# Graph-network kernel, convolution at seven points: VectorE's and ScalarE's order of work in each period and in the first group's preparation rearranged

## The reference, cut to what matters

```python
# layer 0
h = relu(bn1(conv1d(xc, conv1_w, 0)))                  # xc = x transposed, one tap
x_conv = relu(bn2(conv1d(h, conv2_w, 8)) + xc)          # 17 taps
s = x @ w_se.T + b_se                                   # 3 columns
A = exp(-(sq[:, :, None] + sq[:, None, :] - 2 * s @ s.T)) * adj
x_nmp = A @ relu(x @ w_msg.T + b_msg)
gi = concat([x_conv, x_nmp]) @ w_ih.T + b_ih
gh = x @ w_hh.T + b_hh                                  # three gates each: r, z, n
r, z = sigmoid(gi_r + gh_r), sigmoid(gi_z + gh_z)
x = layernorm(x + (1 - z) * tanh(gi_n + r * gh_n) + z * x)
# layer 1
h = relu(((1 + eps) * x + adj @ x) @ W1 + b1)
x = layernorm(x + h @ W2 + b2)
```

## Time and profile before

| | us |
|---|---|
| median of 3 runs | 428.92 (428.90 to 428.99) |
| the profiled execution, its own time | 428.78 |
| its span, first to last instruction | 427.0 |
| TensorE matmuls busy | 371.3 (87%) |
| VectorE busy | 315.6 (74%) |
| ScalarE busy | 226.4 (53%) |
| GpSimd busy | 208.2 (49%) |
| mean granted TensorE clock | 0.982 of full |

### The profile page before, as it was taken

The page is one execution under the profiler, slowest core; times in us unless marked ns, Lnnn a source line. Parts: engine busy times, 40 slices in busy tenths (PEclk is TensorE's granted clock), DMA queues, the critical chain, the costliest instruction groups (busy, mean ns, idle before and its releaser), DMA issues.

```text
span 427.0 us, 6485 instructions
## 1 busy us (share of the span) xinstructions
PE 371.3 (87%) x2191; PEld 321.3 (75%) x2191; DVE 315.6 (74%) x671; ACT 226.4 (53%) x421; POOL 208.2 (49%) x195
## 2 busy tenths in 40 slices
PE   3798699889987999789988899879997899898974
PEld 2577688779775987779777797769886797778864
DVE  5999986778777686768767787776957687774574
ACT  3324546455745367453763557553674537533674
POOL 4729522556227562368325661285523583256243
PEclk9799699999999999999999999999999999999999
DMA  7400021020012010120110200120101201000011
GB/s 248 165 1 2 0 100 50 6 94 26 26 49 100 2 51 0 51 98 0 49 49 8 90 25 25 49 98 2 50 2 49 100 2 51 1 2 0 2 49 49
DMA packets 7991, 19.39 MB, mean 45 GB/s; under 512 B 672, under 2 KB 5024, under 8 KB 6944
## 3 DMA queue, kind: packets, MB, share of 16 engines
q1 hardware_dynamic: 7536, 18.50, 12.2%
q10 hardware_dynamic: 432, 0.59, 0.4%
HBM read 14.90 MB, written 4.19 MB: 45 GB/s over the span
## 4 chain that ended last, share of the span: by engine, by line
PE 30%; DVE 24%; issue 20%; POOL 13%; ACT 11%; DMA 1%; DVEq 0%; ACTq 0%; POOLq 0%; SPq 0%
PE back L1213 16%; POOL rstd L515 4%; PE back L1309 4%; PE conv L1213 4%; PE back L1398 3%; DVE bv L858 3%; DVE xn L1005 3%; POOL av L494 2%; POOL av L492 2%; DVE usum L918 2%; DVE usum L949 2%; ACT amat L656 2%; POOL sv L502 2%; DVE stats L983 1%; DVE msg L880 1%
## 5 line engine op out<-in xcount | busy, mean ns | idle before, releaser
L1213 PE MATMUL conv<-sth,wh 128*128 128x256 f32 x238 | 74.8, 314 | 5.3 <-issue 5.3
L1213 PE MATMUL conv<-stl,wh 128*128 128x256 f32 x238 | 69.0, 290 | 0.0
L1213 PE MATMUL conv<-sth,wl 128*128 128x256 f32 x238 | 68.8, 289 | 0.0
L520 POOL TENSOR_TENSOR xw<-xw,xv 128x512 f32<-128x512 f32 (+1 forms) x17 | 20.8, 1224 | 83.2 <-ACT xw L680 83.2
L515 POOL TENSOR_TENSOR rstd<-rstd,minus_half 128x4 f32<-128x4 f32 (+1 forms) x34 | 34.2, 1006 | 54.9 <-DVE rstd L987 54.9
L533 POOL TENSOR_TENSOR amat<-amat,adjT 128x512 f32<-128x512 f32 x32 | 48.2, 1528 | 16.7 <-ACT amat L656 16.7
L1213 PEld LDWEIGHTS conv<-sth,wh 128*128 128x128 f32 x238 | 46.2, 194 | 7.1 <-issue 5.6
L1213 PEld LDWEIGHTS conv<-stl,wh 128*128 128x128 f32 x238 | 46.4, 195 | 0.5
L1213 PEld LDWEIGHTS conv<-sth,wl 128*128 128x128 f32 x238 | 46.1, 194 | 0.0
L614 ACT ACTIVATE sth<-sv 128x272 fp32r<-128x272 f32 (+1 forms) x35 | 18.1, 518 | 36.3 <-DVE sv L834 21.7
L1309 PE MATMUL back<-adjT,xn 128*128 128x256 f32 x120 | 29.9, 392 | 5.8 <-DVE xn L1005 5.8
(11 more groups left out here) (219 smaller groups left out, 1019.2 us busy)
## 6 DMA issues: line engine op xcount, KB each, us to landing
adjT<-in_adj_dram SPq DMA_DIRECT2D x8, 1024.0 KB, 4.9
out_dram<-tail SPq DMA_DIRECT2D x15, 256.0 KB, 2.2
xv<-in_x_dram SPq DMA_DIRECT2D x7, 512.0 KB, 3.3
gbuf<-in_gates_dram SPq DMA_DIRECT2D x1, 576.0 KB, 6.5
tail<-in_conv_dram ACTq DMA_DIRECT2D x2, 256.0 KB, 3.9
xv<-in_x_dram SPq DMA_DIRECT2D x2, 256.0 KB, 4.6
later_w<-in_later_dram SPq DMA_DIRECT2D x1, 452.0 KB, 6.3
tail<-in_conv_dram SPq DMA_DIRECT2D x1, 320.0 KB, 5.2
```

What stands on the lines that cost most here:

```text
L520: done(pool.tensor_tensor(xw[:, h, part(c)], xw[:, h, part(c)], xv[u][:, part_cols(h, c)], ALU.mult), XWX_READY)
L1213: ins = pe.matmul(bank, a, b, start=first and k == 0, stop=last and k == len(todo) - 1)
```

## The change

The number of instructions of each engine stays as it was, but for two copies that go from VectorE to ScalarE; all else is order. SyncE's list is untouched; GpSimd's and TensorE's change in the preparation alone.

- Every period, VectorE: `messages` and `factors` come ahead of `parts1`, and `u_sum` stands behind `inf_stream`, ahead of `gates(gb, 1)`; `gates_end(gb, 0)` comes ahead of `stream_low(gm, 3)`; `gates_end(gb, 1)` and `y_apply(gb, 0)` and `y_stats(gb, 1)` ahead of `pair2_sum`; `stream_low(gm, 4)` and `pair2_add` behind `y_apply(gb, 1)`; `h_low(gb, 0)` ahead of `pair1_sum`; both `x_low` ahead of both `pair1_add`.
- Every period, ScalarE: `xconv_high(gm, 0)` stands behind the four `hidden` instead of ahead of `exps` 2 and 3.
- Preparation: the two copies of the last tap (L1085, L1086) go to ScalarE with a semaphore of their own; on VectorE the sums of the +2 and -2 taps, the messages, factors, streams and low parts stand in another order; the low parts of w1, MINUS2, MINUS1 and INF go into the first period, around `gates_end(0, 0)` and behind `y_stats(0, 0)`. TensorE's first taps go HALF, ZERO, PLUS2, MINUS2 (which was behind `factors`), and INF ahead of `nmp(0, 0)`. TensorE's first `gates` wait for the low part of the gate weights (w1's before), and its taps MINUS2 for all low parts, as before.

```diff
-        W_ORDER = ("conv1", ZERO, HALF, PLUS2, PLUS1, "gates", "w1", MINUS2, MINUS1, INF)
+        W_ORDER = ("conv1", HALF, ZERO, PLUS2, PLUS1, "gates", "w1", MINUS2, MINUS1, INF)
...
 # GpSimd, prologue
                 pool.wait_ge(pads_zeroed, 2)
+                token_diffs(0, 1)
+                streams2(0)
                 pool.wait_ge(conv2_loaded, 64)
                 pool.tensor_tensor(ataps[:, 10:14, :], c2raw[:, 0:16:4, :], c2raw[:, 2:16:4, :],
                                    ALU.add).then_inc(tap_sums_one, 1)
-                token_diffs(0, 1)
...
-                streams2(0)
...
 # ScalarE, prologue
+                act.wait_ge(conv2_loaded, 64)
+                last_tap = c2raw[:, TAPS - 1:TAPS, :]
+                act.activation(gtaps[:, 4:15:5, :], last_tap.to_broadcast([P, 3, P]), ACT.Copy).then_inc(tap_copies, 1)
+                act.activation(ataps[:, 4:10:5, :], last_tap.to_broadcast([P, 2, P]), ACT.Copy).then_inc(tap_copies, 1)
...
 # ScalarE, steady
-                xconv_high(gm, 0)
                 exps(gm, 2)
                 exps(gm, 3)
                 hidden(gb, 0)
                 hidden(gb, 1)
+                xconv_high(gm, 0)
...
 # VectorE, prologue
-                dve.tensor_copy(gtaps[:, 4:15:5, :], last_tap.to_broadcast([P, 3, P])).then_inc(tap_sums, 1)
-                dve.tensor_copy(ataps[:, 4:10:5, :], last_tap.to_broadcast([P, 2, P])).then_inc(tap_sums, 1)
...
+                tap_low(PLUS1)
+                w_low_part(wl[:, S_GATE:S_GATE + 9, :], graw, wh[:, S_GATE:S_GATE + 9, :], w_count("gates"))
...
-                tap_low(MINUS2)
-                tap_low(MINUS1)
-                tap_low(INF)
 
             def steady(s, u, front):
                 gb, gm, gf = s - 1, s, s + 1
-                parts1(gm)
-                u_sum(gm, u)
+                first = isinstance(s, int) and s == 1
                 for k in range(3):
                     messages(gm, k)
                 factors(gm)
+                parts1(gm)
                 gates(gb, 1 - u, 0)
+                if first:
+                    w_low_part(w1l[:, :], w1raw, w1h[:, :], w_count("w1"))
+                    tap_low(MINUS2)
+                gates_end(gb, 0)
                 stream_low(gm, 3)
-                gates_end(gb, 0)
                 inf_stream(gm)
+                u_sum(gm, u)
                 gates(gb, 1 - u, 1)
                 y_stats(gb, 0)
-                pair2_sum(gm)
+                if first:
+                    tap_low(MINUS1)
+                    tap_low(INF)
                 gates_end(gb, 1)
                 y_apply(gb, 0)
+                y_stats(gb, 1)
+                pair2_sum(gm)
+                y_apply(gb, 1)
+                stream_low(gm, 4)
                 pair2_add(gm)
-                y_stats(gb, 1)
-                stream_low(gm, 4)
-                y_apply(gb, 1)
+                h_low(gb, 0)
                 pair1_sum(gm)
-                h_low(gb, 0)
                 h_low(gb, 1)
-                pair1_add(gm, 0)
                 if front:
                     x_low(gf, 1 - u, 0)
                     x_low(gf, 1 - u, 1)
+                pair1_add(gm, 0)
                 pair1_add(gm, 1)
...
 # TensorE, prologue
+                first_taps(HALF)
                 first_taps(ZERO)
-                first_taps(HALF)
                 first_taps(PLUS2)
+                first_taps(MINUS2)
                 pe.wait_ge(consts_loaded, 16)
                 factors(0)
-                first_taps(MINUS2)
...
+                first_taps(INF)
                 nmp(0, 0)
-                first_taps(INF)
                 nmp(0, 1)
...
 # TensorE, steady
                 if first:
-                    pe.wait_ge(w_low, w_count("w1"))
+                    pe.wait_ge(w_low, w_count("gates"))
```

More of the change, by code:

```diff
@@ L314, in gnn_kernel @@
         tap_sums_one = sem("tap_sums_one")
+        tap_copies = sem("tap_copies")
         def wait(eng, name, g, j):
@@ L723, in prologue @@
                 h1_out(0, 1)
[L724 removed]
+                act.wait_ge(tap_copies, 2)
+                act.wait_ge(tap_sums, 3)
+                tap_high(HALF)
                 tap_high(ZERO)
[L726 to L727 removed]
+                x_high(1, 1)
+                act.wait_ge(tap_sums, 6)
+                tap_high(PLUS2)
                 for k in range(3):
                     msg_out(0, k)
[L730 to L732 removed]
+                act.wait_ge(tap_sums_one, 3)
+                tap_high(PLUS1)
                 factors_out(0)
+                minus2_out(0)
                 exps(0, 0)
                 exps(0, 1)
[L736 removed]
+                act.wait_ge(gates_loaded, 16)
+                act.activation(wh[:, S_GATE:S_GATE + 9, :], graw, ACT.Copy).then_inc(w_high, 1)
                 exps(0, 2)
                 exps(0, 3)
[L739 to L742 removed]
                 act.activation(w1h[:, :], w1raw, ACT.Copy).then_inc(w_high, 1)
@@ L746, in prologue @@
                 h1_out(1, 1, True)
+                act.wait_ge(tap_sums, 7)
+                tap_high(MINUS2)
                 xconv_high(0, 0)
@@ L753, in prologue @@
                 xconv_high(0, 1)
-                act.wait_ge(tap_sums, 9)
-                tap_high(MINUS2)
                 act.wait_ge(tap_sums_one, 4)
@@ L1032, in out_shift, with w_low_part, tap_low @@
                                               ALU.mult, ALU.mult), SHIFT_READY)
+            def w_low_part(dst, src, hi, k):
+                dve.wait_ge(w_high, k)
+                dve.tensor_tensor(dst, src, full(hi), ALU.subtract).then_inc(w_low, 1)
+            def tap_low(n):
+                k = SLOT[(n, 0)]
+                w_low_part(wl[:, k:k + NTAP[n], :], traw[n], wh[:, k:k + NTAP[n], :], w_count(n))
             def prologue():
@@ L1095, in prologue @@
                     messages(0, k)
-                taps_step(utaps[:, 0:4, :], w2, 4.0, w0)
-                taps_step(ataps[:, 5:9, :], w3, 4.0, w1)
-                taps_step(gtaps[:, 5:9, :], ataps[:, 5:9, :], 2.0, utaps[:, 0:4, :])
+                factors(0)
                 taps_step(ataps[:, 5:9, :], ataps[:, 5:9, :], -2.0, utaps[:, 0:4, :])
                 parts1(0)
-                factors(0)
-                tap_low(ZERO)
-                tap_low(HALF)
+                inf_stream(0)
+                x_low(1, 1, 0)
+                x_low(1, 1, 1)
                 dve.wait_ge(tap_sums, steps[0])
                 u_sum(0, 0)
-                x_low(1, 1, 0)
-                x_low(1, 1, 1)
-                tap_low(PLUS2)
-                inf_stream(0)
                 pair2_sum(0)
+                tap_low(HALF)
+                tap_low(ZERO)
                 pair2_add(0)
-                tap_low(PLUS1)
-                w_low_part(wl[:, S_GATE:S_GATE + 9, :], graw, wh[:, S_GATE:S_GATE + 9, :], w_count("gates"))
-                w_low_part(w1l[:, :], w1raw, w1h[:, :], w_count("w1"))
                 pair1_sum(0)
                 pair1_add(0, 0)
+                tap_low(PLUS2)
                 pair1_add(0, 1)
@@ L1119, in prologue @@
                 zero_stream(1)
-                xconv_low(0, 0)
                 stream_low(1, 0)
@@ L1242, in first_taps @@
                 elif n == HALF:
-                    pe.wait_ge(tap_sums, 5)
+                    wait(pe, E_READY_H, 0, 1)
+                    pe.wait_ge(tap_copies, 2)
+                    pe.wait_ge(tap_sums, 3)
                 elif n == PLUS2:
                     wait(pe, R2_READY, 0, 2)
-                    pe.wait_ge(tap_sums, 8)
+                    pe.wait_ge(tap_sums, 6)
                 elif n == MINUS2:
-                    pe.wait_ge(tap_sums, 9)
+                    pe.wait_ge(tap_sums, 7)
                 elif n == PLUS1:
```

31 lines of the change are left out of this document (8 added, 23 removed).

## The result

The changed kernel takes **397.35 us** (396.49 to 398.25, four executions) against 428.96 (428.90 to 429.50, four) on the same chip: a ratio of **0.926, 95% interval 0.923 to 0.929**. The forecast was 399.0 in 393 to 407. The profiled execution took 396.49, with a span of 394.7 and a mean granted clock of 0.990; the span before was 427.0.

The account below looks back on a forecast made before the run. TensorE's list plus its waits, 4.55 us in a steady period, was taken to bound the kernel. 428.78 - 29.0 (periods) - 4.7 (preparation) + 3.8 (first period) = 398.9, hence 399.0 us, in 393 to 407.

Parts of the forecast that it names:

- the periods: All periods together: TensorE's 31.1 us of waits go, less a new 0.3 us wait seven times: -29.0 us.
- the preparation: Before the periods: VectorE's first stream of group 1 starts at 39.8 instead of 44.47, -4.7 us (bounds -2.5 and -5.5).
- the first period: Low parts moved into it make TensorE wait before taps MINUS2: +3.8 us (bounds 2.8, 5).
- The new wait at the first INF tap: In a period, TensorE waits for INF's `stl`, now behind pair 1's xn: 0.3 us, bounds 0 and 0.6.
- step 6: From `conv1(gf, 1)` to the next messages: order unchanged, and TensorE follows without a gap as before.
- Steps 1 and 2: Pair 0's gates lose their 0.81 to 0.93 us wait; moved VectorE work makes L969 0.2 us late, with no TensorE wait.
- Step 3: Before the transpose of pair 1's y: TensorE's 1.51 us wait goes, with 0.9 us to spare.
- Step 5: At `mlp1`: the 1.45 us wait before the fourth tile goes; `x_low` and `pair1_add` have over 1 us to spare.
- VectorE becomes the bound: Rival: moved `parts1` and `u_sum` delay the path to the transposes by 4.86 us each period, 433 us; slower: 0.04.
- No wait stayed off another cause: Rival: `mlp1` or the gates still wait for something else, 404 to 409 us; chance 0.19 shared with ports.
- GpSimd's masks did not hold the preparation to 402: Rival: GpSimd's masks set the preparation's pace, so it gives only -2.5 us: 402 us; no separate chance given.
- The port rival: VectorE's moved `pair2_add` and GpSimd hold each other up, delaying `h_low` before `mlp1`: 406 us; 0.19 shared with one wait left.

Follow-up runs that it names:

- experiment 5: The changed kernel with only `pair2_sum` put back ahead of `gates_end(gb, 1)` on VectorE: 410.43 us, ratio 0.956.
- Experiment 4: The changed kernel with only `parts1` and `u_sum` put back ahead of the messages on VectorE: 402.0 us, ratio 0.937.
- experiment 7: The changed kernel with only `pair1_add(gm, 0)` put back ahead of both `x_low` on VectorE: 400.83 us, ratio 0.934.
- experiment 1: The kernel before with the change's order in the periods only, its preparation kept: 395.54 us, ratio 0.922.
- experiment 11: The changed kernel with the first period's low parts spread and the preparation's -2 taps sum ahead of the messages: 394.83 us, ratio 0.921.

## Why the prediction was right, and where its terms were off

The mechanism was right: the waits named in the earlier trace rows went, and the time went with them. That the total came so near is in part luck, since the terms were off in both directions: the periods gave 3.6 us more than forecast in the spans, the preparation 1.2 more, and the first period cost 2.3 more.

- *The bound* was read rightly. TensorE's list sets the period; take its waits away and the period shrinks by them.
- *The periods* were forecast at -29.0 us, with a mark every 45.2 to 45.4. Alone they gave 33.5 (32.6 in the spans of the profiled executions), a mark every 44.8 to 44.9. The new wait at the first INF tap came and was rightly sized: about 0.2 us for 0.3, though it is in no list. Two things were mis-sized. A removed wait gives more than its listed length: some 5.5 us in a period for the 4.55 listed, 1.7 for 1.5 in experiment 5. And a second new wait of some 0.5 us, before the second `HALF` taps, was not foreseen: step 6 had TensorE without a gap there.
- *Steps 1 and 2* held. Experiment 4 puts the order of messages and `parts1` at 4.7 us in all, though its wait in the first period is 2.0 us shorter, so at some 6.7 us by itself, or 0.96 in each period; the earlier trace rows list 0.8 to 0.9. `parts1` takes 1.14 us in its new place. I had taken 2.21 as its time beside GpSimd, and its cost fell by half for free.
- *Step 3* was right in its sign, its spare was not: 0.53 us and not 0.9 (L982 ends at 163.13, the transpose starts at 163.66), and the spare of the whole VectorE list was nothing. The step looked at each wait alone; a delay on VectorE meets the nearest of all following ones.
- *Step 5* was right in the changed kernel and gave a wrong idea of what each reorder is worth. I had priced `xconv_high` at the 1.45 us of the wait it removes. Undone alone it costs 3.3 us for each period, since `pair1_add` has moved behind `x_low`, and undone with it 3.0, part of which is the clock; at the upper clock it is 3.0 and 1.8 us. The reorders depend on each other. "Over 1 us to spare" for `x_low` was wrong too: it takes 3.40 us for two instead of the 1.28 of before, and experiment 7 shows TensorE waiting for it when it starts 1.6 us later.
- *The preparation* was forecast at -4.7 us, with the stream at 39.8 and the first split tap near 42. They came at 40.22 and 41.99, 4.25 and 4.73 us earlier than before. TensorE stood still 2.64 us and not the 3.4 of the forecast. The clock fell, as taken, but came back sooner: 0.55 over 3.6 us where the earlier trace rows have 0.50 over 5.9. That is about 1.1 us more. With the first gates' wait (0.36 by the first mark of experiment 1, 62.94 against 63.30) it makes the 6.2 us of the first mark. The masks started 2.1 us earlier, at 28.34, and not 2.5; the 0.7 us for ScalarE's copy (0.69 measured) was as worked out. What was missed is the 3.20 us wait before the -2 taps. It was named ("hold TensorE too"), and its size was not.
- *The first period* was forecast at +3.8 us (2.8 to 5). The wait was 4.59 us, and the clock fell behind it, which the text had left out of the sum as a coin toss against a gain in the preparation. In all this period is 6.1 us longer than a steady one (50.97 less 44.8), against the 3.8; the 1.5 us over the wait is about what the 16 tap matmuls at 0.213 us apart instead of 0.125 make (1.4). In proportion this term was furthest off, in the other direction from the periods.
- *The rivals.* That VectorE becomes the bound was given a price of 433 and a point of 0.9 us. The point was too far off: TensorE already waits for VectorE's list in every period, and 0.98 us of added work costs 6.7 us. The price needed 4.86 us of it in each period, and nothing near that came, so the 0.04 for slower is not shown to be too low. No wait stayed off another cause, and GpSimd's masks did not hold the preparation to 402. The port rival was half right, and in another place. `pair2_add` was not slowed (two sums of 0.69). GpSimd's sum beside them was, 2.60 us against 1.27 just before, and VectorE's `x_low` beside the masks takes 3.40 for two:

```profile
168.24 0.69 DVE L941 TENSOR_TENSOR usum<-usum,pm 128x512 f32<-128x512 f32 x1
168.84 0.69 DVE L942 SCALAR_TENSOR_TENSOR usum<-pm,usum 128x512 f32<-128x512 f32 x1
...
172.00 3.40 DVE L820 TENSOR_TENSOR xl<-xv,xh 128x512 fp32r<-128x512 f32 x2
```

```profile
166.54 1.27 POOL L528 TENSOR_TENSOR tail<-xn,later_w 128x512 f32<-128x512 f32 x1
168.05 2.60 POOL L528 TENSOR_TENSOR tail<-xn,later_w 128x512 f32<-128x512 f32 x1 [0.24 <-DVE xn L1010]
170.62 5.91 POOL L534 TENSOR_TENSOR amat<-amat,adjT 128x512 f32<-128x512 f32 x4
```

  VectorE is then busy without a gap up to the low part of the second `HALF` taps, which come some 0.5 us later than before the change. That the slow `x_low` is the cause is argued from these rows; no run takes it alone. The wait is so short that it is listed in two periods only (0.25 and 0.29 us):

```profile
183.98 0.38 PE L1217 MATMUL conv<-sth,wh 128*128 128x256 f32 x1 [0.29 <-DVE stl L820]
```

  In experiment 7 the same stretch of TensorE, from `conv1`'s start to these taps, is 9.07 us instead of 9.62. The Trainium skill (SBUF — State Buffer, "SBUF: two separate sides") says that whichever of GpSimd and a VectorE operation with two inputs in SBUF starts first keeps the shared ports for its whole instruction. The rows agree that one of the two holds the other up; which one pays changes from instruction to instruction, here within 4 us. The 406 us that the rule led to did not come: `x_low` took 2.1 us more than before, and only about 0.5 us of that can have reached TensorE.

What stays open: why the two parts of the change add to less than their sum is shown in the first period's wait and clock, but the share of the 3.2 us wait in the preparation was not separated; experiment 11 moved it and gained nothing.

## What to carry to other kernels

When an engine list is rearranged to remove waits of the bounding engine, price the list of the engine it waited for from end to end, too: its smallest spare anywhere decides how near it is to being the bound, and one added instruction measures that. Price a wait from start to start of the waiting engine's instructions, too: here a list of waits left out two that came in every period, and gave the removed ones some 0.2 us too short each. Work that is moved out of an early stage into a place covered by waits costs its full length once the same change removes those waits. And undo reorders one by one before believing a price: two that move the same instruction past each other aren't worth the sum of their waits.
